# Softmax attention on one core: scores in three single PSUM banks, row maxima in three, exponentials 512 wide

## The chip, the core and the metric

The program runs on one core of one Trainium2 chip. A core has five engines with an instruction stream each: TensorE (PE, matrix multiplications and transposes), VectorE (DVE), ScalarE (ACT), GpSimd (POOL) and SyncE (SP, which issues the DMAs here). They wait for each other by semaphores. TensorE writes its results to PSUM, which has 8 banks of 512 fp32 words for each of 128 partitions, and VectorE and ScalarE read them there. The metric is the device time of the whole program in microseconds (us), less is better.

## The reference, cut to what matters

Four blocks follow one another on x of 2048 rows by 128 columns. Only the first, a softmax attention with 16 heads of width 8, is touched by the change:

```
x = x + _L0_attn_a_ref(_layernorm(x), w_qkv, w_out, b_out)
x = x + _L0_ffn_ref(...)          # six layers, local attention and MLP
x = x + _L0_attn_b_ref(...)       # linear attention
x = x + _L0_ffn_ref(...)          # the six layers again

def _L0_attn_a_ref(x, w_qkv, w_out, b_out):
    q, k, v = ...                 # x @ w_qkv, split in 16 heads of width 8
    q = _apply_rope(q, cos, sin)
    k = _apply_rope(k, cos, sin)
    scores = jnp.einsum('bhqd,bhkd->bhqk', q, k) / math.sqrt(D_HEAD)
    probs = jax.nn.softmax(scores, axis=-1)
    out = jnp.einsum('bhqk,bhkd->bhqd', probs, v)
    return out.transpose(...).reshape(b, t, d) @ w_out + b_out
```

Each head therefore has a matrix of 2048 by 2048 scores, whose rows each have their maximum subtracted before the exponential.

## The kernel before

`softmax_attention` makes the score matrix of each head twice. The first pass has the queries on the partitions: `scores_for_max` (L528) multiplies 128 queries by 512 keys into a bank of `ps_max`, and `maximum` (L413, on DVE) reduces it to one column. 64 such pairs, m = 0 to 63, make a head; `negate` (L418) turns the maxima into extra rows of the query operand, so that the second pass yields scores with the maximum already taken off. The second pass has the keys on the partitions: `scores` (L533) multiplies 128 keys by 512 queries, again 64 matmuls i = 0 to 63 in each head. ACT takes the exponential (L340) into `pex`, and `values` (L543) multiplies that by the values of the head, which adds up both the output and the denominator in the bank `ps_o`. An eighth bank, `ps_t`, serves the transposes of operands (`first`, `second`), which ACT copies out (L328, L333), and of the sums (`turn_sums`).

A head is 32 steps, n = 0 to 31. Two steps belong to one tile of 128 keys, kt = n // 2. In this text the two steps of a tile are called a group, so a head has groups 0 to 15. PE's stream in a group, written out by hand in `head` (L562), is: a maximum matmul, two scores, two maximum matmuls, two scores, a maximum matmul, the four `values` matmuls of the previous key tile. We call the scores of a group s1 to s4 and its maxima m1 to m4. The maxima belong to a later head: up to n = 25 to the next one (from its twelfth pair on), from n = 26 on to the one after that. In groups 8 to 11 the odd step (n = 17, 19, 21, 23, table `FIRST`) ends with eight transposes of the operands of head h + 2, and ACT copies them after its exponentials of that step. Steps 29 and 30 (`SECOND`) do the same for the query operand of head h + 1. Step 5 ends with `turn_sums`; on DVE `sums(h-1)` stands ahead of the maxima of step 2, `negate` ahead of those of step 26 and `outputs(h-1)` behind those of step 6.

What sets the pace between the engines is the number of free PSUM banks. `ps_max` has two banks, so matmul m waits until DVE has reduced m - 2 (L529). `ps_s` has two buffers of two banks. ACT reads one buffer, 1024 columns, with one instruction, and a pair of score matmuls waits for the exponential of the pair two steps back (L536). `pex` has two buffers, one for each key tile in work, and an exponential waits for the `values` of two tiles back (L339).

Head 0 and heads 13 to 15 are written out; heads 1 to 12 are three rounds of a hardware loop with four heads each (L192), in which the numbers that the engines wait for are computed in registers. Ahead of head 0 stands a preparation in which the 64 maxima of head 0 and the first 12 of head 1 are made with nothing beside them (L592 and L597). In head 14 the maxima end with step 25 and there are no `FIRST` transposes; in head 15 there are no maxima at all.

Of the kernel before, what the change touches and what calls it, by code (L numbers as in the profile page):

```python
# [7 lines left out]
F32 = mybir.dt.float32  # L8
BF16 = mybir.dt.bfloat16
ALU = mybir.AluOpType  # L10
ACT = mybir.ActivationFunctionType
AX = mybir.AxisListType

P = 128
D = 128
N = 2048
NT = N // P
# [14 lines left out]
NG = NT // GT  # L32
# [66 lines left out]
def softmax_attention(nc, tag, x_in, w_qkv, w_out, b_out, consts, x_out, xf, xa):  # L99


    with ExitStack() as ctx:
# [6 lines left out]
            sems.append(ctx.enter_context(nc.semaphore(f"{tag}_{name}")))  # L109
            return sems[-1]  # L110

        ps_s = [ctx.enter_context(nc.psum_tensor(f"{tag}_scores{i}", [P, 2, 512], F32)) for i in range(2)]
        ps_max = [ctx.enter_context(nc.psum_tensor(f"{tag}_max{i}", [P, 512], F32)) for i in range(2)]
        ps_o = ctx.enter_context(nc.psum_tensor(f"{tag}_sums", [P, 512], F32))
        ps_t = ctx.enter_context(nc.psum_tensor(f"{tag}_turned", [P, 512], F32))
        quarter = [ps_s[i // 2][:, i % 2, :] for i in range(4)]

        GQ = GT * P
        wqkv = sb("wqkv", [P, 3 * D])
# [22 lines left out]
        stackT = sb("stackT", [P, 4, 2, N], BF16)  # L142
        v_head = sb("v_head", [P, 2, NT, VW])
        maxima = sb("maxima", [P, NT, 4])
        neg = sb("neg", [P, 3, NT])
        pex = sb("pex", [P, 2, NG, GQ])
# [18 lines left out]
        own = {e: sem(f"own_{e}") for e in ("pool",)}  # L165

        PASS, STEPS = 4 * NT, 2 * NT


        EARLY = 12  # L170
# [125 lines left out]

        @block.scalar
        def _(act):
            act.sem_inc(act_ex, 2)

            def put_xT(g):
                act.wait_ge(pe_xT, g + 1)
                if g >= 2:
                    act.wait_ge(pe_qkv, g - 1)
                act.copy(xnT[:, g % 2, :, :], ps_t[:].rearrange("p (s q) -> p s q", s=GT)).then_inc(act_xT, 1)

            put_xT(0)
            for g in range(NG):
                if g + 1 < NG:
                    put_xT(g + 1)  # L310
                act.wait_ge(pe_qkv, g + 1)
                if g >= 2:
                    act.wait_ge(pl_t1, 2 * g - 2)
                    act.wait_ge(dv_t2, 4 * g - 4)
                for s in range(GT):
                    last = act.copy(qk[:, g % 2, :, s, :], quarter[s][:, 0:2 * D].rearrange("p (k d) -> p k d", k=2))
                last.then_inc(act_qk, 1)
                for s in range(GT):
                    last = act.copy(v_all[:, g * GT + s, :], quarter[s][:, 2 * D:3 * D])
                last.then_inc(act_v, 1)  # L320

            act.wait_ge(ld_c, 80)
            act.copy(ident_bf[:], ident[:]).then_inc(act_ident, 1)

            def first(h, slot, n):

                act.wait_ge(pe_first, 4 * h + n + 1)
                act.copy(stackT[:, slot, 1 - n // 2, 1024 * (n % 2):1024 * (n % 2) + 1024], ps_t[:].bitcast(BF16)).then_inc(act_first, 1)  # L328

            def second(h, slot, n):  # L330

                act.wait_ge(pe_second, 2 * h + n + 1)
                act.copy(stackT[:, slot, 0, 1024 * n:1024 * n + 1024], ps_t[:].bitcast(BF16)).then_inc(act_second, 1)  # L333

            def head(h, u):
                for n in range(STEPS):
                    kt, j = n // 2, n % 2
                    act.wait_ge(pe_s, STEPS * h + (n + 1))
                    act.wait_ge(pe_pv, NT * h + (kt + 1))  # L339
                    act.activation(pex[:, kt % 2, 2 * j:2 * j + 2, :], ps_s[j][:], ACT.Exp).then_inc(act_ex, 1)  # L340
                    if n in FIRST and exists(h, 2):
                        first(h + 2, (u + 2) % 4, FIRST[n])
                    if n in SECOND and exists(h, 1):
                        second(h + 1, (u + 1) % 4, SECOND[n])

            for h in range(2):
                for n in range(4):
                    first(h, h, n)
            for n in range(2):
                second(0, 0, n)  # L350
            all_heads(act, head)
            for g in range(NG):
                act.wait_ge(pe_aT, g + 1)
                if g >= 2:
                    act.wait_ge(pe_y, g - 1)
                act.copy(aoT[:, g % 2, :, :], ps_t[:].rearrange("p (s q) -> p s q", s=GT)).then_inc(act_aT, 1)

        @block.vector
        def _(dve):
            dve.sem_inc(dv_max, 2)  # L360
            dve.sem_inc(dv_os, 1)

            def norm_stats(k, g):
# [49 lines left out]
            def maximum(h, m):  # L413

                dve.wait_ge(pe_max, PASS * h + (m + 1))
                dve.tensor_reduce(maxima[:, m // 4, m % 4:m % 4 + 1], ps_max[m % 2][:], AX.X, ALU.max).then_inc(dv_max, 1)  # L416

            def negate(h, p):  # L418

                dve.wait_ge(dv_max, PASS * h + (PASS + 2))  # L420
                dve.tensor_reduce(neg[:, 0, :], maxima[:], AX.X, ALU.max, negate=True).then_inc(dv_neg, 1)
                dve.wait_ge(pe_first, 4 * h + 4)
                for i in range(3):
                    dve.wait_ge(dv_neg, 3 * h + (i + 1))
                    at = stack[:, p, 0, :, 72 + i]
                    dve.tensor_copy(at, neg[:, i, :]).then_inc(dv_negp, 1)
                    if i < 2:
                        dve.wait_ge(dv_negp, 3 * h + (i + 1))
                        dve.tensor_tensor(neg[:, i + 1, :], neg[:, i, :], at, ALU.subtract).then_inc(dv_neg, 1)
# [49 lines left out]
        def _(pe):  # L479
# [46 lines left out]
                transposes(p, 0, n).then_inc(pe_second, 1)  # L526

            def scores_for_max(h, slot, m):  # L528
                pe.wait_ge(dv_max, PASS * h + (m + 1))  # L529
                pe.matmul(ps_max[m % 2][:], stackT[:, slot, 0, P * (m // 4):P * (m // 4) + P],  # L530
                          stackT[:, slot, 1, GQ * (m % 4):GQ * (m % 4) + GQ], start=True, stop=True).then_inc(pe_max, 1)

            def scores(h, slot, n):  # L533

                kt, j = n // 2, n % 2
                pe.wait_ge(act_ex, STEPS * h + (n + 1))  # L536
                for e in range(2):
                    g = 2 * j + e
                    last = pe.matmul(ps_s[j][:, e, :], stackT[:, slot, 1, P * kt:P * kt + P],  # L539
                                     stackT[:, slot, 0, GQ * g:GQ * g + GQ], start=True, stop=True)  # L540
                last.then_inc(pe_s, 1)

            def values(h, p, kt):  # L543

                pe.wait_ge(act_ex, STEPS * h + (2 * kt + 4))
                if kt == 0:
                    pe.wait_ge(dv_os, h + 1)
                for g in range(NG):
                    last = pe.matmul(ps_o[VW * g:VW * g + VW, :], v_head[:, p, kt, :], pex[:, kt % 2, g, :],  # L549
                                     start=(kt == 0), stop=(kt == NT - 1), tile_position=(0, VW * g))  # L550
                last.then_inc(pe_pv, 1)
# [1129 lines left out]
```

## Time and profile before

| | |
|---|---|
| median of 3 runs | 5906.45 us (5892.85 to 5911.36) |
| profiled execution | 5901.95 us, its span 5900.1 us |
| granted TensorE clock, mean of the span | 0.955 |
| softmax attention, maxima of the preparation | 80.75 to 139 us of the span |
| softmax attention, the 16 heads | 139.8 to 993.4 us of the span |
| PE, DVE, ACT busy in the whole span | 87%, 75%, 65% |
| DVE maxima (L416) | 1024 of 686 ns |
| ACT exponentials (L340) | 512 of 1026 ns |

All times in the rows below are counted from the start of the span. A duration that a row gives for PE is that of one matmul from its start to its last write, and matmuls overlap: what a matmul costs PE is the distance between two starts. PEld is the loading of the weights ahead of a matmul. The rest of the program, from about 1000 us to the end, is code that the change doesn't touch.

### The profile page before, as it was taken

How to read it: one execution, taken by the hardware profiler on the slowest of the kernel's cores; microseconds unless marked ns; L12 is line 12 of the kernel's file. 1: busy time of each engine (PE TensorE's matmuls, PEld its weight loads, DVE VectorE, ACT ScalarE, POOL GpSimd, SP SyncE). 2: the span in 40 equal slices, each digit the busy share in tenths (PEclk: the TensorE clock that was granted, in tenths of full speed). 3: DMA queues.
4: the chain of work that ended last, by engine and by line, in shares of the span. 5: the costliest groups of instructions: out<-in, count | busy, mean ns of one | idle time of the engine just before them, and what ended most of it. 6: DMA issues, size and time to landing. Idle time of an engine off the chain costs nothing. (4 is left out here: it accounts for less than half of the span.)

```text
span 5900.1 us, 135041 instructions
## 1 busy us (share of the span) xinstructions
PE 5113.0 (87%) x38884; PEld 3411.9 (58%) x38884; DVE 4421.2 (75%) x8097; ACT 3864.6 (65%) x11648; POOL 2938.9 (50%) x2878
## 2 busy tenths in 40 slices
PE   5999997898988989989889677989989889898897
PEld 1223222566666666666666455666666666666665
DVE  7777775786876868868778546868868778687785
ACT  1666665775776757757667405757757677577675
POOL 3000000665665656656566306656656566566564
PEclk6999999999999999999999868999999999999999
DMA  0000001212222221121221202122222221212223
GB/s 12 1 1 1 1 1 38 60 48 70 52 58 58 52 70 47 48 73 48 68 54 47 75 9 82 48 69 53 60 57 49 69 52 47 73 49 60 59 51 85
DMA packets 332293, 288.23 MB, mean 49 GB/s; under 512 B 149102, under 2 KB 290708, under 8 KB 329748
## 3 DMA queue, kind: packets, MB, share of 16 engines
q1 hardware_dynamic: 331028, 282.33, 18.6%
q8 instruction: 222, 3.64, 0.3%
q14 instruction: 275, 2.25, 0.1%
q10 hardware_dynamic: 768, 0.02, 0.0%
HBM read 100.81 MB, written 30.41 MB: 22 GB/s over the span
## 5 line engine op out<-in xcount | busy, mean ns | idle before, releaser
L416 DVE TENSOR_REDUCE a_maxima<-a_max 128x1 f32<-128x512 f32 x1024 | 652.2, 686 | 195.8 <-PE a_max L530 191.8
L985 ACT ACTIVATE g_ex<-g_bank,g_nmx 128x96 f32<-128x96 f32 x1536 | 501.4, 338 | 345.3 <-DVE g_nmx L1067 345.3
L985 ACT ACTIVATE f_ex<-f_bank,f_nmx 128x96 f32<-128x96 f32 x1536 | 501.4, 338 | 343.1 <-DVE f_nmx L1067 343.1
L340 ACT ACTIVATE a_pex<-a_scores 128x1024 f32<-128x1024 f32 x512 | 517.1, 1026 | 217.4 <-PE a_scores L539 208.7
L920 POOL TENSOR_TENSOR f_rn<-f_sg,f_minus_half 128x8 f32<-128x8 f32 x384 | 640.1, 1667 | 32.0
L920 POOL TENSOR_TENSOR g_rn<-g_sg,g_minus_half 128x8 f32<-128x8 f32 x384 | 639.7, 1666 | 32.0
L925 POOL TENSOR_TENSOR f_qr<-f_t 128x512 f32<-128x512 f32 x384 | 547.7, 1426 | 14.8 <-DVE f_t L1086 13.1
L925 POOL TENSOR_TENSOR g_qr<-g_t 128x512 f32<-128x512 f32 x384 | 537.2, 1399 | 14.8 <-DVE g_t L1086 13.1
L1162 PE MATMUL g_bank<-g_wqkv,g_xT 128*128 128x512 f32 x768 | 427.7, 640 | 87.2 <-DVE g_qh L1077 62.1
L1162 PE MATMUL f_bank<-f_wqkv,f_xT 128*128 128x512 f32 x768 | 427.5, 639 | 86.6 <-DVE f_qh L1077 61.7
L530 PE MATMUL a_max<-a_stackT 128*128 128x512 bf16 x1024 | 410.9, 402 | 57.1 <-DVE a_maxima L416 26.2
L1061 DVE TENSOR_TENSOR g_pn<-g_ex,g_rd 128x384 f32<-128x384 f32 x384 | 426.7, 1111 | 13.1
L917 POOL TENSOR_SCALAR g_sg<-g_ss 128x8 f32<-128x8 f32 x384 | 92.4, 241 | 649.1 <-DVE g_ss L1073 649.1
L917 POOL TENSOR_SCALAR f_sg<-f_ss 128x8 f32<-128x8 f32 x384 | 92.3, 240 | 645.7 <-DVE f_ss L1073 645.7
L1061 DVE TENSOR_TENSOR f_pn<-f_ex,f_rd 128x384 f32<-128x384 f32 x384 | 393.3, 1024 | 13.1
L1067 DVE TENSOR_REDUCE f_nmx<-f_bank 128x4 f32<-128x384 f32 x384 | 212.1, 552 | 254.5 <-PE f_bank L1180 254.5
L1180 PEld LDWEIGHTS f_bank<-f_kT,f_qbd 128*128 128x128 f32 x3072 | 392.9, 192 | 8.0 <-issue 4.0
L1180 PEld LDWEIGHTS g_bank<-g_kT,g_qbd 128*128 128x128 f32 x3072 | 392.9, 192 | 8.0 <-issue 4.0
L1180 PE MATMUL f_bank<-f_kT,f_qbd 128*128 128x96 f32 x3072 | 394.6, 272 | 0.0
L1180 PE MATMUL g_bank<-g_kT,g_qbd 128*128 128x96 f32 x3072 | 394.6, 272 | 0.0
L1067 DVE TENSOR_REDUCE g_nmx<-g_bank 128x4 f32<-128x384 f32 x384 | 211.3, 550 | 227.6 <-PE g_bank L1180 227.6
L273 POOL COPY a_v_head<-a_v_all 128x128 f32 (+1 forms) x16 | 4.6, 290 | 738.3 <-PE a_sums L549 738.3
(235 smaller groups left out, 13205.3 us busy)
## 6 DMA issues: line engine op xcount, KB each, us to landing
f_vw<-f_vt SPq DMA_DIRECT2D x96, 384.0 KB, 4.3
g_vw<-g_vt SPq DMA_DIRECT2D x96, 384.0 KB, 4.3
f_vw<-f_vt SPq DMA_DIRECT2D x96, 256.0 KB, 3.6
g_vw<-g_vt SPq DMA_DIRECT2D x96, 256.0 KB, 3.6
f_vw<-f_vt SPq DMA_DIRECT2D x96, 128.0 KB, 2.3
g_vw<-g_vt SPq DMA_DIRECT2D x96, 128.0 KB, 2.3
f_wqkv<-in_f_Wqkv_dram SPq DMA_DIRECT2D x7, 1536.0 KB, 7.3
g_wqkv<-in_f_Wqkv_dram SPq DMA_DIRECT2D x7, 1536.0 KB, 9.4
```

What stands on the lines that cost most here:

```text
L273: pool.tensor_copy(v_head[:, p, :, 0:AD], one(v_all, h)).then_inc(pl_vh, 1)
L340: act.activation(pex[:, kt % 2, 2 * j:2 * j + 2, :], ps_s[j][:], ACT.Exp).then_inc(act_ex, 1)
L416: dve.tensor_reduce(maxima[:, m // 4, m % 4:m % 4 + 1], ps_max[m % 2][:], AX.X, ALU.max).then_inc(dv_max, 1)
L530: pe.matmul(ps_max[m % 2][:], stackT[:, slot, 0, P * (m // 4):P * (m // 4) + P], stackT[:, slot, 1, GQ * (m % 4):GQ * (m % 4) + GQ], start ...
L917: pool.tensor_scalar(sg[:, b, :], ss[:, b, :], 1e-24, None, ALU.max).then_inc(pl_sg, 1)
L920: pool.tensor_tensor(rn[:, b, :], sg[:, b, :], minus_half[:], ALU.pow).then_inc(pl_rn, 1)
L925: pool.tensor_tensor(qr[:, 1 - b, :], t1[:, 1 - b, :], t2[:, 1 - b, :], ALU.add).then_inc(pl_qr, 1)
L985: last = act.activation(ex[:, b, u, :], ps_s[:, KEYS * u:KEYS * u + KEYS], ACT.Exp, bias=nmx[:, b, u:u + 1], accum_out=sm[:, b, u:u + 1])
L1061: dve.tensor_tensor(pn[:, 1 - b, :, :], ex[:, 1 - b, :, :], rd[:, 1 - b, :].unsqueeze(2).broadcast_to([P, 4, KEYS]), ALU.mult).then_inc(dv ...
L1067: dve.tensor_reduce(nmx[:, b, :], ps_s[:, 0:4 * KEYS].rearrange("p (u c) -> p u c", u=4), AX.X, ALU.max, negate=True).then_inc(dv_max, 1)
L1162: pe.matmul(ps_qk[b][:], xT[:, q, :], wqkv[:, at:at + 512], start=True, stop=True).then_inc(pe_qkv, 1)
L1180: last = pe.matmul(ps_s[:, KEYS * u:KEYS * u + KEYS], qbd[:, j, blk, :], kT[:, j, BLK * blk:BLK * blk + KEYS], start=False, stop=(u == 3))
```

## The change

Eight banks are dealt out anew. The scores get three buffers of one bank (`ps_s`), the maxima get three (`ps_max`), the sums and the transposes keep one each. `quarter`, the four banks that the projections ahead of and behind the heads use, becomes the three score banks and the first maxima bank. ACT makes each exponential with an instruction of its own over 512 columns, 1024 instructions in place of 512, and each increments `act_ex`; so each of the 64 score matmuls of a head waits for the exponential that frees its bank, and each signals ACT by itself. Score i of a head uses bank i mod 3, so it waits for exponential i - 3; as 64 isn't a multiple of 3, `freed` gives the first three of a head their own numbers. The maxima go by the same function. The semaphores' starting values and the counts in `values` and `negate` follow. The numbers of instructions of PE's and DVE's work, and their sizes, stay.

```
@@ -109,11 +109,11 @@
             sems.append(ctx.enter_context(nc.semaphore(f"{tag}_{name}")))
             return sems[-1]
 
-        ps_s = [ctx.enter_context(nc.psum_tensor(f"{tag}_scores{i}", [P, 2, 512], F32)) for i in range(2)]
-        ps_max = [ctx.enter_context(nc.psum_tensor(f"{tag}_max{i}", [P, 512], F32)) for i in range(2)]
+        ps_s = [ctx.enter_context(nc.psum_tensor(f"{tag}_scores{i}", [P, 512], F32)) for i in range(3)]
+        ps_max = [ctx.enter_context(nc.psum_tensor(f"{tag}_max{i}", [P, 512], F32)) for i in range(3)]
         ps_o = ctx.enter_context(nc.psum_tensor(f"{tag}_sums", [P, 512], F32))
         ps_t = ctx.enter_context(nc.psum_tensor(f"{tag}_turned", [P, 512], F32))
-        quarter = [ps_s[i // 2][:, i % 2, :] for i in range(4)]
+        quarter = [ps_s[0][:], ps_s[1][:], ps_s[2][:], ps_max[0][:]]
 
         GQ = GT * P
         wqkv = sb("wqkv", [P, 3 * D])
@@ -166,6 +166,12 @@
 
         PASS, STEPS = 4 * NT, 2 * NT
 
+        AHEAD = 20 * PASS
+
+        def freed(h, i):
+
+            return PASS * h + ((0, -2, -1)[i] if i < 3 else i - 2)
+
 
         EARLY = 12
         LATE = (PASS - EARLY) // 2
@@ -296,7 +302,7 @@
 
         @block.scalar
         def _(act):
-            act.sem_inc(act_ex, 2)
+            act.sem_inc(act_ex, AHEAD)
 
             def put_xT(g):
                 act.wait_ge(pe_xT, g + 1)
@@ -334,10 +340,12 @@
 
             def head(h, u):
                 for n in range(STEPS):
-                    kt, j = n // 2, n % 2
-                    act.wait_ge(pe_s, STEPS * h + (n + 1))
-                    act.wait_ge(pe_pv, NT * h + (kt + 1))
-                    act.activation(pex[:, kt % 2, 2 * j:2 * j + 2, :], ps_s[j][:], ACT.Exp).then_inc(act_ex, 1)
+                    kt = n // 2
+                    if n % 2 == 0:
+                        act.wait_ge(pe_pv, NT * h + (kt + 1))
+                    for i in (2 * n, 2 * n + 1):
+                        act.wait_ge(pe_s, PASS * h + (i + 1))
+                        act.activation(pex[:, kt % 2, i % NG, :], ps_s[i % 3][:], ACT.Exp).then_inc(act_ex, 1)
                     if n in FIRST and exists(h, 2):
                         first(h + 2, (u + 2) % 4, FIRST[n])
                     if n in SECOND and exists(h, 1):
@@ -357,7 +365,7 @@
 
         @block.vector
         def _(dve):
-            dve.sem_inc(dv_max, 2)
+            dve.sem_inc(dv_max, PASS)
             dve.sem_inc(dv_os, 1)
 
             def norm_stats(k, g):
@@ -413,11 +421,11 @@
             def maximum(h, m):
 
                 dve.wait_ge(pe_max, PASS * h + (m + 1))
-                dve.tensor_reduce(maxima[:, m // 4, m % 4:m % 4 + 1], ps_max[m % 2][:], AX.X, ALU.max).then_inc(dv_max, 1)
+                dve.tensor_reduce(maxima[:, m // 4, m % 4:m % 4 + 1], ps_max[m % 3][:], AX.X, ALU.max).then_inc(dv_max, 1)
 
             def negate(h, p):
 
-                dve.wait_ge(dv_max, PASS * h + (PASS + 2))
+                dve.wait_ge(dv_max, PASS * h + 2 * PASS)
                 dve.tensor_reduce(neg[:, 0, :], maxima[:], AX.X, ALU.max, negate=True).then_inc(dv_neg, 1)
                 dve.wait_ge(pe_first, 4 * h + 4)
                 for i in range(3):
@@ -526,23 +534,22 @@
                 transposes(p, 0, n).then_inc(pe_second, 1)
 
             def scores_for_max(h, slot, m):
-                pe.wait_ge(dv_max, PASS * h + (m + 1))
-                pe.matmul(ps_max[m % 2][:], stackT[:, slot, 0, P * (m // 4):P * (m // 4) + P],
+                pe.wait_ge(dv_max, freed(h + 1, m))
+                pe.matmul(ps_max[m % 3][:], stackT[:, slot, 0, P * (m // 4):P * (m // 4) + P],
                           stackT[:, slot, 1, GQ * (m % 4):GQ * (m % 4) + GQ], start=True, stop=True).then_inc(pe_max, 1)
 
             def scores(h, slot, n):
 
-                kt, j = n // 2, n % 2
-                pe.wait_ge(act_ex, STEPS * h + (n + 1))
-                for e in range(2):
-                    g = 2 * j + e
-                    last = pe.matmul(ps_s[j][:, e, :], stackT[:, slot, 1, P * kt:P * kt + P],
-                                     stackT[:, slot, 0, GQ * g:GQ * g + GQ], start=True, stop=True)
-                last.then_inc(pe_s, 1)
+                kt = n // 2
+                for i in (2 * n, 2 * n + 1):
+                    g = i % NG
+                    pe.wait_ge(act_ex, AHEAD + freed(h, i))
+                    pe.matmul(ps_s[i % 3][:], stackT[:, slot, 1, P * kt:P * kt + P],
+                              stackT[:, slot, 0, GQ * g:GQ * g + GQ], start=True, stop=True).then_inc(pe_s, 1)
 
             def values(h, p, kt):
 
-                pe.wait_ge(act_ex, STEPS * h + (2 * kt + 4))
+                pe.wait_ge(act_ex, PASS * h + (AHEAD + 4 * kt + 4))
                 if kt == 0:
                     pe.wait_ge(dv_os, h + 1)
                 for g in range(NG):
```

In head 0 PE's instructions of the first two steps stand as follows before (the digit behind `a_max` and `a_scores` is the buffer; a `scores` buffer holds two banks here).

```order
L530 MATMUL a_max0<-a_stackT 128x512 [waits a_dv_max,a_pl_vh,a_act_second]
L539 MATMUL a_scores0<-a_stackT 128x512 [waits a_act_ex]
L539 MATMUL a_scores0<-a_stackT 128x512
L530 MATMUL a_max1<-a_stackT 128x512 [waits a_dv_max]
L530 MATMUL a_max0<-a_stackT 128x512 [waits a_dv_max]
L539 MATMUL a_scores1<-a_stackT 128x512 [waits a_act_ex]
L539 MATMUL a_scores1<-a_stackT 128x512
L530 MATMUL a_max1<-a_stackT 128x512 [waits a_dv_max]
```

And the same place in the changed kernel, where each buffer is one bank.

```order
L538 MATMUL a_max0<-a_stackT 128x512 [waits a_dv_max,a_pl_vh,a_act_second]
L547 MATMUL a_scores0<-a_stackT 128x512 [waits a_act_ex]
L547 MATMUL a_scores1<-a_stackT 128x512 [waits a_act_ex]
L538 MATMUL a_max1<-a_stackT 128x512 [waits a_dv_max]
L538 MATMUL a_max2<-a_stackT 128x512 [waits a_dv_max]
L547 MATMUL a_scores2<-a_stackT 128x512 [waits a_act_ex]
L547 MATMUL a_scores0<-a_stackT 128x512 [waits a_act_ex]
L538 MATMUL a_max0<-a_stackT 128x512 [waits a_dv_max]
```

No matmul changes its place in PE's order. The third maximum no longer goes into the bank of the first, the fourth score goes into the bank of the first score of the same group, and every score has a wait.

ACT's instructions at the start of head 0, behind the last two copies of the preparation, before:

```order
L333 COPY a_stackT<-a_turned 128x1024 [waits a_pe_second] x2
L340 ACTIVATE a_pex<-a_scores0 128x1024 [waits a_pe_pv,a_pe_s]
L340 ACTIVATE a_pex<-a_scores1 128x1024 [waits a_pe_pv,a_pe_s]
L340 ACTIVATE a_pex<-a_scores0 128x1024 [waits a_pe_pv,a_pe_s]
L340 ACTIVATE a_pex<-a_scores1 128x1024 [waits a_pe_pv,a_pe_s]
```

And in the changed kernel:

```order
L339 COPY a_stackT<-a_turned 128x1024 [waits a_pe_second] x2
L348 ACTIVATE a_pex<-a_scores0 128x512 [waits a_pe_s,a_pe_pv]
L348 ACTIVATE a_pex<-a_scores1 128x512 [waits a_pe_s]
L348 ACTIVATE a_pex<-a_scores2 128x512 [waits a_pe_s]
L348 ACTIVATE a_pex<-a_scores0 128x512 [waits a_pe_s]
L348 ACTIVATE a_pex<-a_scores1 128x512 [waits a_pe_s,a_pe_pv]
L348 ACTIVATE a_pex<-a_scores2 128x512 [waits a_pe_s]
```

Four instructions take the place of two in each group, and the wait for `values` stands at the first of the four alone.

## Rows read from the trace of the kernel before

**Rows 1.** Stages: preparation, head 3, head 15.

```profile
core 0: us, PE busy (x) PEld busy (x) DVE busy (x) ACT busy (x) POOL busy (x), PEclk, DMA share, GB/s
80.75:139.00 58.25, 47.48 (x93) 9.49 (x93) 50.34 (x83) 2.61 (x3) 2.86 (x7) 0.50 0.00 0
...
302.40:357.00 54.60, 51.25 (x309) 16.48 (x308) 42.85 (x74) 37.73 (x39) 3.15 (x8) 1.00 0.00 1
...
959.60:993.40 33.80, 32.79 (x194) 6.64 (x194) 1.24 (x3) 30.96 (x32) 0.00 (x0) 1.00 0.00 1
```

**Rows 2.** Waits, 240 to 820 us: total us, times, longest us.

```profile
PEld a_max L530 <- DVE a_maxima L416: 247.4, 424, 1.5
```

**Rows 3.** Timeline, group 5 of head 3: start us, us long, engine, instruction, [idle before].

```profile
324.26 0.39 PE L530 MATMUL a_max<-a_stackT 128*128 128x512 bf16 x1
...
324.48 0.59 PE L539 MATMUL a_scores<-a_stackT 128*128 128x512 bf16 x2
324.68 2.53 DVE L416 TENSOR_REDUCE a_maxima<-a_max 128x1 f32<-128x512 f32 x4 [0.61 <-PE a_max L530]
...
324.91 0.91 PE L530 MATMUL a_max<-a_stackT 128*128 128x512 bf16 x2
325.19 2.12 ACT L340 ACTIVATE a_pex<-a_scores 128x1024 f32<-128x1024 f32 x2 [1.02 <-PE a_scores L539]
...
325.66 0.59 PE L539 MATMUL a_scores<-a_stackT 128*128 128x512 bf16 x2
...
326.09 0.38 PE L530 MATMUL a_max<-a_stackT 128*128 128x512 bf16 x1
...
326.40 1.07 PE L549 MATMUL a_sums<-a_pex,a_v_head 128*32 128x512 f32 x8
...
327.40 0.39 PE L530 MATMUL a_max<-a_stackT 128*128 128x512 bf16 x1
```

**Rows 4.** ACT by line and shape: busy us, mean ns | idle before us.

```profile
L340 ACT ACTIVATE a_pex<-a_scores 128x1024 f32<-128x1024 f32 x512 | 517.1, 1026 | 217.4 <-PE a_scores L539 208.7
...
L976 ACT ACTIVATE g_sq<-g_bank 128x512 f32<-128x512 f32 x384 | 235.3, 613 | 112.8 <-PE g_bank L1162 112.8
...
L328 ACT COPY a_stackT<-a_turned 128x1024 bf16<-128x1024 bf16 x64 | 64.8, 1012 | 76.9 <-PE a_turned L504 76.9
...
L305 ACT COPY a_xnT<-a_turned 128x512 f32<-128x512 f32 x4 | 2.5, 635 | 12.3 <-PE a_turned L487 12.3
...
L356 ACT COPY a_aoT<-a_turned 128x512 f32<-128x512 f32 x4 | 2.3, 585 | 7.6 <-PE a_turned L608 7.6
```

**Rows 5.** Timeline of group 9 of head 3, behind a set of transposes.

```profile
331.00 0.38 PE L530 MATMUL a_max<-a_stackT 128*128 128x512 bf16 x1
...
331.20 1.01 ACT L328 COPY a_stackT<-a_turned 128x1024 bf16<-128x1024 bf16 x1 [0.74 <-PE a_turned L504]
...
332.11 1.95 ACT L340 ACTIVATE a_pex<-a_scores 128x1024 f32<-128x1024 f32 x2
...
334.13 0.62 PE L504 MATMUL a_turned<-a_ident_bf,a_stack 128*128 128x128 bf16 x8
...
334.58 0.38 PE L530 MATMUL a_max<-a_stackT 128*128 128x512 bf16 x1
```

**Rows 6.** Timeline of PE: starts of groups 1 and 2, of 13 and 14.

```profile
304.62 0.39 PE L530 MATMUL a_max<-a_stackT 128*128 128x512 bf16 x1
...
308.06 0.39 PE L530 MATMUL a_max<-a_stackT 128*128 128x512 bf16 x1
...
344.89 0.39 PE L530 MATMUL a_max<-a_stackT 128*128 128x512 bf16 x1
...
348.76 0.39 PE L530 MATMUL a_max<-a_stackT 128*128 128x512 bf16 x1
```

**Rows 7.** Timeline of PE in the preparation.

```profile
98.22 1.21 PE L530 MATMUL a_max<-a_stackT 128*128 128x512 bf16 x2 [0.18 <-DVE a_maxima L416]
...
101.01 1.21 PE L530 MATMUL a_max<-a_stackT 128*128 128x512 bf16 x2 [0.18 <-DVE a_maxima L416]
```

## The prediction

> **What bounds the kernel now.** I read the table of stages first [rows 1]. A head takes 54.60 us, in which PE is busy for 51.25, DVE for 42.85 and ACT for 37.73. No engine but PE comes near the length of the head, so the question is what PE waits for. The list of waits names it [rows 2]: in 580 us the weight loads of the maxima matmuls ended their idle time 424 times on a DVE reduction, far ahead of anything else on PE. (The 247.4 us there are idle time of the weight loader and not of the matmuls, so they are no price.) The price stands in the timeline of one ordinary group [rows 3]. It begins with m1 at 324.26, and the next begins at 327.40: 3.14 us. PE's starts lie 0.22 us apart (two scores in 0.43), 0.31 ahead of `values`, and 1.00 behind it. One step is longer. The two maxima merged at 324.91 last 0.91 together and one lasts 0.39, so m3 starts at 325.43, which is 0.52 after m2 in place of 0.22. It waits for the reduction of m1, which starts at 324.68 and lasts 0.69 (0.686 in the kernel's mean): to 325.37, and PE goes 0.06 later. So 0.30 us of each ordinary group is a wait for one of two maxima banks; without it a group is 2.84 us.
>
> ACT isn't tight there. Its two exponentials take 2.12 us of the 3.14, the second starting 0.04 after the last score ended (325.66 + 0.59 = 326.25, against 325.19 + 2.12 - 1.02 = 326.29).
>
> **The change, part by part.** *Third maxima bank.* m3 no longer waits for m1 but for the reduction of the previous group's m4. The four reductions of a group follow each other every (2.53 - 0.69) / 3 = 0.61 us, 2.4 us in a group of 2.84, so DVE keeps up and the 0.30 goes. What is late next is to be looked for at the scores.
>
> *Exponentials of 512 columns.* The trace has no exponential of that size. The copy of 1024 columns takes 1012 ns and one of 512 takes 585 [rows 4], which is 0.83 ns for each column; 1026 - 427 gives 0.60 us. Back to back, the two behind the copy take 1.95 us at 1.03 each [rows 5], so the second starts 0.92 after the first; 512 columns less make this 0.49. Bounds: 0.585, the shortest operation of this width in rows 4, and 1.026, the whole exponential as it is. The squares of 512 columns take 613 and the copies of the preparation 635, both close to the lower end, so I take 0.60. ACT then needs 4 x 0.49 to 4 x 0.60 = 2.0 to 2.4 us in a group, which is still under 2.84: 512 additional instructions cost nothing as long as PE doesn't wait for one.
>
> The Trainium skill speaks against this part. "Advanced Engine Details and Errata", section TRN2 Errata, says that each ScalarE instruction exposes its access latency as a bubble, and advises large tiles and reading several PSUM banks with one instruction, which is what the change gives up. "ScalarE: Activation LUTs", section What ACT_TABLE_LOAD costs, gives 186 ns + 0.833 ns for each column, 0.613 us here and 93 ns less in series: by an estimate from that page each round trip below is 0.013 longer, about 3 us over the heads.
>
> *Three score banks, each with its own wait.* s4 goes into the bank of s1 of its own group. Without any stall s4 stands 0.22 + 5 x 0.22 = 1.31 us after m1 (rounded steps: 0.22, 0.44, 0.65, 0.87, 1.09, 1.31). The bank comes free like this: s1 starts at 0.22 and lasts 0.38, ACT starts 0.04 later and takes 0.60, and PE goes 0.06 later, at 1.30. That is just in time, so an ordinary group is 2.84, but with no reserve: each further 0.01 in this trip is 0.01 in each group. The wait at each score costs PE nothing in itself. Maxima matmuls have such a wait and a register operation of their own now, and where the bank is free they stand 0.22 apart like the rest [rows 3].
>
> *Groups behind a copy (9 to 12).* Here the trip is longer. The copy starts 0.20 after m1 and the next exponential 0.91 after the copy [rows 5]. s4 can go at 0.20 + 0.91 + 0.60 + 0.06 = 1.77, 0.46 late. In groups 9 to 11 the transposes then close a ring: from the copy's start 1.57 to s4, 0.22 to m4, 0.31 to `values`, 1.00 to the transposes, 0.62 for these, 0.04 to the next copy, 3.76 us in all. Before it is 334.58 - 331.00 = 3.58. Each of the three costs 0.18, and group 12 costs 0.46 - 0.30 = 0.16.
>
> *The rest of a head.* Groups 0, 2 to 8 and 14 gain 0.30 each, 2.70. Group 1, where DVE copies the sums ahead of its maxima, takes 308.06 - 304.62 = 3.44 [rows 6] and becomes 2.84, since the bank it waits for is freed 0.6 earlier: 0.60. Group 13 has `negate` ahead of its maxima and takes 348.76 - 344.89 = 3.87, that is a stall of 3.87 - 2.84 = 1.03 at m3. The stall moves to m4, 0.65 further on in PE's order, and 0.38 is left: 0.65 gained. At the end of a head s64 and s1 of the next head share a bank. From the first `SECOND` copy ACT needs 0.91 + 2 x 0.49 + 0.91 + 0.49 + 0.60 = 3.89 until the bank is free, while PE reaches s1 after 1.01 + 0.06 + 0.46 + 3 x 0.22 + 0.31 + 1.00 + 0.22 = 3.72: 0.23 lost. (0.46 is what eight transposes cost PE, 334.58 - 334.13.) Sum of a head: -2.70 - 0.60 - 0.65 + 3 x 0.18 + 0.16 + 0.23 = -3.02. Heads 0 to 13: -42.3.
>
> *Head 14* has no `FIRST`. Groups 0 to 12 gain 12 x 0.30 + 0.60 = 4.2. Groups 13 to 15 have no maxima and lose about 0.4 + 0.4 + 0.6 to the trip of the next item: -2.8.
>
> *Head 15* has scores, exponentials and `values` alone. It takes 33.80 us [rows 1], ACT busy for 30.96, 2.11 a group. With three banks s4 must be followed by `values` and then by the next s1 before ACT gets work: 0.31 + 1.00 + 0.38 + 0.04 + 0.60 + 0.06 = 2.39, since the next s4 needs that exponential. 16 x 2.39 = 38.2: +4.4.
>
> *Preparation.* Two banks, four matmuls every 101.01 - 98.22 = 2.79 us [rows 7], so 0.70 for each maximum, at a granted clock of 0.50 [rows 1], the 1.2 GHz level. The trip of one bank is 0.61 (matmul) + 0.04 + 0.69 + 0.06 = 1.40. Over three banks this is 0.47, below DVE's own 0.61. 76 x 0.09 = 6.8 gained.
>
> Sum: -42.3 - 2.8 + 4.4 - 6.8 = **-47.5 us**. The profiled execution took 5901.95 us, 1.85 around its span of 5900.1; with the change 5854. The median of the runs is 4.5 higher, 5906.45, and gives 5859. I forecast **5858 us**. The other four stages, from 1000 us on, have the same code.
>
> **Rivals.** *The score trip replaces the bank wait (short gain).* The ordinary group has 0.01 in reserve. If the handoffs with their register operations are longer than I took them (the first exponential in rows 3 starts 0.12 after the scores ended, 325.07 to 325.19, where the second takes 0.04), each group's trip grows by 0.08. Then an ordinary group is 2.91, rows behind copies 3.84, head 15 2.47 a group: 0.08 x 15 groups x 15 heads = 18 back, plus 1.3 in head 15: a gain of 28, **5878**. For it: two handoffs of different length in the same row. Against it: the longer one belongs to an instruction that has two waits, and the changed kernel puts the `values` wait, long fulfilled, ahead of it.
>
> *ACT becomes the bound (slower).* If an exponential of 512 columns costs nearly as much as one of 1024, since it has a fixed cost, a bubble and a wait of its own, ACT sets the pace. A head has 64 of them and 6 copies of 1.01. At 0.80 us each this is 51.2 + 6.1 = 57.3 against 54.60, +2.7 in 15 heads; head 15 becomes 51.2 against 33.80, +17.4; the preparation gives 6.8 back: +51, **5957**. It decides from about 0.75 us on: 15 heads x (48.0 + 6.1 - 54.6) + 14.2 - 6.8 = 0. For it stands the first rule of the skill above. Against it: everything of 512 columns in rows 4 lies at 0.59 to 0.64.
>
> *The third maxima bank gives nothing (no change).* DVE's next reduction, not the bank, could hold m3. It would have to be busy, and it idles 0.61 us ahead of m1's reduction in each group [rows 3]. Should half of the stall stay, as a wait at m3 or m4, 0.15 x 11 groups x 15 heads = 25 of the 47.5 is lost, **5881**. With all of it left the price of the copies and of head 15 stands alone against the preparation, and the time is about 5904.
>
> **How the numbers follow.** Forecast 0.75. Short gain 0.13. No change 0.07, ACT as the bound 0.05. The forecast's own range, from exponentials of 0.585 to 0.635 and a few us of scatter between runs, is 5846 to 5870; with the short gain the range is **5845 to 5886**. Faster by more than 0.3% (18 us, about what a measurement tells from no change) means under 5889: nearly all of the first two, 0.87. Within 0.3%: 0.08. Slower: 0.05.
>
> **What would show it.** In the changed profile an ordinary group of head 3 should last 2.84 us, with m3 0.22 after m2; the exponentials should have a mean of 0.60 and stand 0.49 apart behind a copy. Groups 9 to 11 should take 3.76, with PE waiting for ACT at s4. Head 3 should last 51.6, head 15 38, the maxima of the preparation 0.61 each. The prediction is wrong if the exponentials take over 0.65, if ordinary groups show PE waiting at s4, or if m3 still starts 0.5 after m2.

## The result and the profile after

| | before | changed |
|---|---|---|
| median | 5908.9 us (4 runs, 5892.85 to 5916.06) | 5856.93 us (4 runs, 5853.8 to 5868.74) |
| profiled execution | 5901.95 us, span 5900.1 | 5853.8 us, span 5852.0 |
| first exponential of head 0 | 139.77 us | 131.66 us |
| end of head 15 | 993.4 us | 945.2 us |
| from there to the end of the span | 4906.7 us | 4906.8 us |

The ratio of the changed kernel to the one before is 0.9913, 95% interval 0.9901 to 0.9926: it is faster, by 52 us in the medians and by 48.1 in the two profiled spans. All of the latter lies in the softmax attention.

The stages, to be read against [rows 1]: maxima of the preparation, head 3, head 15 of the changed kernel.

```profile
core 0: us, PE busy (x) PEld busy (x) DVE busy (x) ACT busy (x) POOL busy (x), PEclk, DMA share, GB/s
80.72:131.00 50.28, 41.55 (x93) 9.20 (x92) 46.24 (x82) 2.61 (x3) 2.87 (x7) 0.64 0.00 0
286.00:337.40 51.40, 49.63 (x309) 16.58 (x308) 43.05 (x74) 38.55 (x70) 3.17 (x8) 1.00 0.00 1
905.80:945.20 39.40, 34.31 (x195) 7.68 (x193) 1.24 (x3) 33.02 (x64) 0.00 (x0) 1.00 0.00 1
```

A head of the loop went from 54.6 to 51.4 us, and PE, busy for 49.63 of them, has 1.8 us without work left in place of 3.4. Head 15 is the stage that became longer, from 33.80 to 39.40.

The waits of the changed kernel from 232 to 780 us (total us, times, longest us) answer to [rows 2].

```profile
PEld a_max L538 <- DVE a_maxima L424: 87.4, 116, 0.8
...
PEld a_scores L547 <- ACT a_pex L348: 73.3, 168, 0.8
...
PE a_scores L547 <- ACT a_pex L348: 12.3, 40, 0.3
```

The maxima's wait for DVE is down from 424 times to 116. The scores' wait for ACT, which isn't among the longest waits of before, is now the second longest of those of PE and its weight loader. As before, the first two lines are idle time of the weight loader and no price; the last one, 40 times 0.3 us, is PE's own and comes from the groups behind a copy, shown below.

One ordinary group of the changed kernel (group 5 of head 2, start and length in us), against [rows 3]:

```profile
248.61 0.39 PE L538 MATMUL a_max<-a_stackT 128*128 128x512 bf16 x1
...
248.84 0.59 PE L547 MATMUL a_scores<-a_stackT 128*128 128x512 bf16 x2
...
249.25 2.06 ACT L348 ACTIVATE a_pex<-a_scores 128x512 f32<-128x512 f32 x4 [0.77 <-PE a_scores L547]
249.27 0.59 PE L538 MATMUL a_max<-a_stackT 128*128 128x512 bf16 x2
...
249.70 0.60 PE L547 MATMUL a_scores<-a_stackT 128*128 128x512 bf16 x2
...
251.44 0.39 PE L538 MATMUL a_max<-a_stackT 128*128 128x512 bf16 x1
```

It lasts 251.44 - 248.61 = 2.83 us, where it was 3.14. The pair m2, m3 now lasts 0.59 and not 0.91: both start 0.22 apart, and no wait is left there. The pair s3, s4 lasts 0.60 where a pair without a wait lasts 0.59, so s4 goes just in time. The exponentials have a mean of 606 ns:

```profile
L348 ACT ACTIVATE a_pex<-a_scores 128x512 f32<-128x512 f32 x1024 | 531.6, 606 | 157.7 <-PE a_scores L547 157.7
```

Group 9 of head 3, which stands behind a copy, has turned into the ring of the prediction; compare [rows 5]. First PE, then ACT.

```profile
311.79 0.38 PE L538 MATMUL a_max<-a_stackT 128*128 128x512 bf16 x1
...
313.56 0.39 PE L547 MATMUL a_scores<-a_stackT 128*128 128x512 bf16 x1 [0.31 <-ACT a_pex L348]
...
315.55 0.38 PE L538 MATMUL a_max<-a_stackT 128*128 128x512 bf16 x1
```

```profile
311.99 1.01 ACT L334 COPY a_stackT<-a_turned 128x1024 bf16<-128x1024 bf16 x1 [0.78 <-PE a_turned L512]
312.90 2.07 ACT L348 ACTIVATE a_pex<-a_scores 128x512 f32<-128x512 f32 x4
315.75 1.01 ACT L334 COPY a_stackT<-a_turned 128x1024 bf16<-128x1024 bf16 x1 [0.77 <-PE a_turned L512]
```

From copy to copy it is 3.76 us, and from m1 to m1 too, where before it was 3.58. s4 starts at 313.56, 1.77 after m1 and 1.57 after the start of the copy.

Head 15, where the loss is (PE and ACT):

```profile
920.57 0.82 PE L547 MATMUL a_scores<-a_stackT 128*128 128x512 bf16 x3
921.06 2.06 ACT L348 ACTIVATE a_pex<-a_scores 128x512 f32<-128x512 f32 x4 [0.39 <-PE a_scores L547]
...
921.71 0.39 PE L547 MATMUL a_scores<-a_stackT 128*128 128x512 bf16 x1 [0.32 <-ACT a_pex L348]
...
923.03 0.82 PE L547 MATMUL a_scores<-a_stackT 128*128 128x512 bf16 x3
```

Three scores go out, the fourth waits for the exponential of the first, and `values` stands between it and the next three: 2.46 us a group. Here s1, the first of the three and 0.39 long, ends at 920.57 + 0.39 = 920.96, and ACT starts 0.10 later. In the group of head 2 above s1 ends at 248.84 + 0.38 = 249.22, and ACT starts 0.03 later (0.04 by the trace's unrounded times).

### The profile page after: what moved, and what is told of

Its sections match the earlier page's. It is cut to its first block and busy times, and to the rows that moved or that the text cites. A ratio compares the mean times of both kernels' runs of the same rounds, so it can differ in the third digit from the quotient of the medians.

```text
span 5852.0 us, 136065 instructions
## 1 busy us (share of the span) xinstructions
PE 5077.2 (87%) x38884; PEld 3412.5 (58%) x38884; DVE 4411.0 (75%) x8097; ACT 3883.6 (66%) x12160; POOL 2947.4 (50%) x2878
## 5 line engine op out<-in xcount | busy, mean ns | idle before, releaser
L348 ACT ACTIVATE a_pex<-a_scores 128x512 f32<-128x512 f32 x1024 | 531.6, 606 | 157.7 <-PE a_scores L547 157.7
L538 PE MATMUL a_max<-a_stackT 128*128 128x512 bf16 x1024 | 365.4, 394 | 14.3 <-DVE a_maxima L424 7.5
```

The costliest lines, as they stand in the source:

```text
L348: act.activation(pex[:, kt % 2, i % NG, :], ps_s[i % 3][:], ACT.Exp).then_inc(act_ex, 1)
L538: pe.matmul(ps_max[m % 3][:], stackT[:, slot, 0, P * (m // 4):P * (m // 4) + P], stackT[:, slot, 1, GQ * (m % 4):GQ * (m % 4) + GQ], start ...
```

## Experiments

The theory is that of the prediction: the third maxima bank brings the gain; exponentials of 512 columns are free in themselves; but with three score banks, the trip of a bank (a score matmul, an exponential and the two handoffs, which are the times from the end of one engine's instruction to the start of the next engine's) must fit into what PE has to do until it needs the bank again, and where it doesn't, PE waits at s4. The main rival says that the narrower exponentials, each freeing its bank early, bring the gain. Each comparison has its own runs of the kernel before: median 5899.67 us (14 runs) for the first four, 5910.21 (18 runs) for the last two. So ratios are compared across them, and single groups by the traces.

### Two maxima banks in the changed kernel

```
-        ps_max = [... for i in range(3)]      # scores keep three banks
+        ps_max = [... for i in range(2)]
-                pe.wait_ge(dv_max, freed(h + 1, m))
-                pe.matmul(ps_max[m % 3][:], ...
+                pe.wait_ge(dv_max, PASS * h + (m + 1))
+                pe.matmul(ps_max[m % 2][:], ...
```

> The changed kernel with two maxima banks again and the eighth bank unused; scores and exponentials stay as changed. Theory (the gain is the third maxima bank): an ordinary group goes from 2.83 back to 3.13 us with m3 0.52 behind m2, groups 9 to 11 stay at 3.76, a head of the loop takes 55.2 in place of 51.4, the maxima of the preparation 0.70 each in place of 0.60. 14 x 3.8 + 4 + 7 = 64 us more than the changed kernel: 5921, which is 12 slower than the kernel before. Rival (the narrower exponentials, each freeing its own bank, bring the gain): ordinary groups stay under 2.95 and the time under 5875.

Measured: 5926.22 us, ratio to before 1.0042 (1.0028 to 1.0056), slower than before by some 25 us. Head 3 and an ordinary group of it, PE's rows:

```profile
305.40:360.90 55.50, 51.25 (x304) 16.46 (x308) 43.27 (x74) 39.63 (x70) 3.17 (x8) 1.00 0.00 1
```

```profile
321.52 0.59 PE L547 MATMUL a_scores<-a_stackT 128*128 128x512 bf16 x2 [0.16 <-issue]
321.95 0.91 PE L538 MATMUL a_max<-a_stackT 128*128 128x512 bf16 x2
...
324.66 0.59 PE L547 MATMUL a_scores<-a_stackT 128*128 128x512 bf16 x2
```

The pair m2, m3 lasts 0.91 again and the group 324.66 - 321.52 = 3.14. The heads as a whole, from the first exponential to the last, take 876.3 us against 813.6 with three maxima banks and 853.7 before. The rival falls: with all of the change but the third maxima bank the kernel is slower than before, by 22.6 us in the heads. This is the price of having three score banks in place of four; the next run takes the narrow exponentials out of it.

### Narrow exponentials alone, over four score banks

```
-        ps_s = [... [P, 2, 512] ... for i in range(2)]
+        ps_s = [... [P, 512] ... for i in range(4)]
-                    act.activation(pex[:, kt % 2, 2 * j:2 * j + 2, :], ps_s[j][:], ...
+                    for i in (2 * n, 2 * n + 1):
+                        act.wait_ge(pe_s, PASS * h + (i + 1))
+                        act.activation(pex[:, kt % 2, i % NG, :], ps_s[i % 4][:], ...
-                pe.wait_ge(act_ex, STEPS * h + (n + 1))          # once for two scores
+                    pe.wait_ge(act_ex, PASS * h + (AHEAD + i - 3))   # for each
```

> The kernel before with the other half of the change alone: exponentials of 512 columns over four single score banks, a wait for each score, two maxima banks. Theory: with a fourth bank no score waits and the narrower instructions hide under PE; ordinary groups stay at 3.14 because m3 still waits for the reduction of m1; head 15 about 1 us shorter; in all 5905 (5898 to 5912), no change. Rival 1 (freeing banks sooner is itself worth something): 5885 or less. Rival 2 (512 more instructions on ACT cost something): over 5920, with ACT late in groups 9 to 12.

Measured: 5903.7 us, ratio 1.0006 (0.9996 to 1.0015). Heads 3 and 15, and the maxima pair of an ordinary group:

```profile
301.70:356.30 54.60, 50.53 (x304) 16.47 (x308) 42.87 (x74) 39.75 (x71) 3.17 (x8) 1.00 0.00 1
959.40:991.50 32.10, 31.28 (x191) 7.70 (x193) 1.24 (x3) 31.70 (x65) 0.00 (x0) 1.00 0.01 1
```

```profile
318.20 0.91 PE L534 MATMUL a_max<-a_stackT 128*128 128x512 bf16 x2
```

Head 3 is what it was, and the heads as a whole take 852.5 us against 853.7. The 512 additional instructions of ACT and the 512 additional waits of PE cost nothing, and they win nothing either, but for head 15, in which ACT was busy for 30.96 of 33.8 us: it takes 32.1, where about 1 us less was expected. Both rivals fall. This kernel and the one of the run above differ in the fourth score bank alone, and in the heads by 876.3 - 852.5 = 23.8 us: groups 9 to 11 of head 3 take 3.59 here and 3.76 there, head 15 32.1 and 39.4.

### The copy behind the first exponential of the next step

```
                     for i in (2 * n, 2 * n + 1):
                         act.wait_ge(pe_s, PASS * h + (i + 1))
                         act.activation(...)
-                    if n in FIRST and exists(h, 2):
-                        first(h + 2, (u + 2) % 4, FIRST[n])
+                        if i == 2 * n and n - 1 in FIRST and exists(h, 2):
+                            first(h + 2, (u + 2) % 4, FIRST[n - 1])
```

> The changed kernel, in which ACT makes each FIRST copy behind the first exponential of the next step and not ahead of it; nothing else moves. Theory (groups 9 to 12 are a ring copy, exponential of s1, s4, values, transposes, copy): s4's bank is free in time again, groups 9 to 11 go from 3.76 to PE's own 3.30 and group 12 keeps its length or loses a little; head 3 goes from 51.4 to 49.7, 14 heads x 1.65 = 23 us: 5834. Rival (these groups are held by the transposes' own bank or by ACT's total work): they stay at 3.7 or more, 5850 to 5860.

Measured: 5830.72 us, ratio 0.9885 (0.9869 to 0.9902). Group 9 of head 3, PE and then ACT:

```profile
306.22 0.38 PE L538 MATMUL a_max<-a_stackT 128*128 128x512 bf16 x1
...
307.30 0.59 PE L547 MATMUL a_scores<-a_stackT 128*128 128x512 bf16 x2
...
309.49 0.38 PE L538 MATMUL a_max<-a_stackT 128*128 128x512 bf16 x1
```

```profile
306.85 0.60 ACT L348 ACTIVATE a_pex<-a_scores 128x512 f32<-128x512 f32 x1 [1.21 <-PE a_scores L547]
307.34 1.01 ACT L334 COPY a_stackT<-a_turned 128x1024 bf16<-128x1024 bf16 x1
308.23 1.60 ACT L348 ACTIVATE a_pex<-a_scores 128x512 f32<-128x512 f32 x3
```

The group takes 309.49 - 306.22 = 3.27 us in place of 3.76, and the pair s3, s4 has no wait. Head 3 takes 49.8, where 49.7 were expected, and the heads 790.9 against 813.6. So the ring is shown, and it was the order on ACT alone that closed it: the copy that nobody needs soon stood ahead of the exponential that frees s4's bank. (Counted from m1 to m1 as here, group 12 becomes shorter too, from 3.30 to 3.01, and group 13 longer, from 3.21 to 3.35.)

### Longer exponentials, in the changed kernel and in the one before

```
-                        act.activation(..., ps_s[i % 3][:], ACT.Exp)
+                        act.activation(..., ps_s[i % 3][:], ACT.Exp, bias=no_bias[:])   # a column of zeros
     # and at the start a memset of that column and one wait for it
```

> The changed kernel with exponentials made longer by a cost of their own: each takes its bias, a zero, from a column in SBUF and not as a constant. The sums are the same. Theory (s4's bank is free just in time, so there is no reserve): whatever x an exponential becomes longer, each ordinary group, each of groups 9 to 11 and each group of head 15 becomes longer by x. With x of about 0.09 us an ordinary group is 2.92, groups 9 to 11 3.85, head 15 2.55 a group; 0.09 x 15 groups x 15 heads + 1.5 = 22 us more than the changed kernel, 5879. Rival (ACT has slack, it is busy for only 70% of the heads, so its instructions may be longer for nothing): 5857.

> The kernel before with the same longer exponentials (of 1024 columns, bias from a column in SBUF). Theory: with four score banks the exponentials have a reserve of several tenths of a us, ordinary groups stay at 3.14 and groups 9 to 11 at 3.59; only head 15, where ACT is the bound, gets 32 x 0.09 = 3 us longer: 5903 to 5910. Rival (longer exponentials cost the same in both kernels, so the loss of the other run isn't due to the missing bank): 20 us more, 5920 or over.

Measured: the changed kernel with longer exponentials 5893.45 us, ratio 0.9976 (0.9967 to 0.9986) against 0.9913 without; the kernel before with them 5915.09, ratio 1.0006 (0.9995 to 1.0017). Both medians lie above the times expected, by 14 and 5 us; the median of the kernel before had itself risen by 10.5 in this comparison, so the theory is judged by the heads. In the trace of the changed one the exponentials have a mean of 692 ns, 0.09 more than 606, and an ordinary group is this:

```profile
305.72 0.59 PE L550 MATMUL a_scores<-a_stackT 128*128 128x512 bf16 x2 [0.16 <-ACT a_pex L351]
...
306.58 0.69 PE L550 MATMUL a_scores<-a_stackT 128*128 128x512 bf16 x2
...
308.64 0.59 PE L550 MATMUL a_scores<-a_stackT 128*128 128x512 bf16 x2
```

The pair s3, s4 lasts 0.69: s4 waits for 0.10. The group is 308.64 - 305.72 = 2.92, so the 0.09 of one exponential appear once in the group, in full. Head 3 takes 53.03, and the heads 837.8 against 813.6, 24.2 more where 22 were expected. (The rest of the difference of the medians isn't from the heads, see the last section.) In the kernel before, with exponentials of 1117 ns:

```profile
319.39 0.59 PE L542 MATMUL a_scores<-a_stackT 128*128 128x512 bf16 x2 [0.16 <-ACT a_pex L343]
319.82 0.91 PE L533 MATMUL a_max<-a_stackT 128*128 128x512 bf16 x2
...
322.53 0.59 PE L542 MATMUL a_scores<-a_stackT 128*128 128x512 bf16 x2
```

The group is 3.14 as ever and heads 1 to 3 take 54.56. Only head 15 reacts, 35.4 against 33.8, which is 1.6 us where 3 were expected. The same 0.09 us cost 24 us in the heads with three score banks (837.8 against 813.6) and 2 with four (855.7 against 853.7).

### All together

```
-        SECOND = {29: 0, 30: 1}
+        SECOND = {28: 0, 30: 1}
     # written-out heads: act.wait_ge(pe_s, ...) first, then act.wait_ge(pe_pv, ...)
+        def score_bank(h, i):
+            return (ps_s + ps_max)[i % 6][:] if last_head(h) else ps_s[i % 3][:]
     # and the moved copy of the run above
```

> As the run with the moved copy, and three more steps: the SECOND transposes and copies at steps 28 and 30 in place of 29 and 30 (so that PE doesn't wait for the first copy ahead of the second transposes); in the written-out heads the wait for values ahead of the exponential is put where the scores' wait is the last one (0.06 us in each group of heads 0, 13, 14, 15); and head 15, which has no maxima, uses the three maxima banks for scores too. Theory: 23 us by the copy, 15 heads x 0.5 = 7 by SECOND, about 2.5 by the waits, 39.4 - 33 = 6 in head 15: 5857 - 38 = 5819. Rival (only the copy counts, PE being full otherwise): 5834.

Measured: 5815.51 us, ratio 0.9862 (0.9846 to 0.9879), the fastest of all, 1.4% under the kernel before. Heads 3 and 15:

```profile
279.00:328.40 49.40, 48.28 (x305) 16.78 (x309) 42.85 (x74) 38.58 (x71) 3.15 (x8) 1.00 0.00 1
873.50:905.60 32.10, 31.09 (x192) 7.72 (x193) 1.24 (x3) 31.65 (x64) 0.00 (x0) 1.00 0.00 1
```

Head 15 goes from 39.4 to 32.1 us with three banks more, the order of its waits included. A loop head goes from 49.8 to 49.3 by `SECOND`. Step three, the order of two waits, shows in an ordinary group of head 13, which is written out. First the run with the moved copy alone, then this one (starts of m1):

```profile
801.65 0.39 PE L538 MATMUL a_max<-a_stackT 128*128 128x512 bf16 x1
...
804.54 0.39 PE L538 MATMUL a_max<-a_stackT 128*128 128x512 bf16 x1
```

```profile
795.16 0.39 PE L547 MATMUL a_max<-a_stackT 128*128 128x512 bf16 x1
...
797.99 0.39 PE L547 MATMUL a_max<-a_stackT 128*128 128x512 bf16 x1
```

2.89 us became 2.83, the length that such a group has in the loop. The other two steps don't touch this group.

The brackets [waits ...] of the `order` lists name the waits of an instruction in the reverse of their order in the program, and so does the expectation when it puts the scores' wait last: in the program this run puts it first, as the lines above say. The kernel before has that order everywhere, and in its written-out heads ACT starts 868.91 - (868.28 + 0.60) = 0.03 us behind the scores (head 13):

```profile
868.28 0.60 PE L539 MATMUL a_scores<-a_stackT 128*128 128x512 bf16 x2
...
868.91 1.02 ACT L340 ACTIVATE a_pex<-a_scores 128x1024 f32<-128x1024 f32 x1 [0.94 <-PE a_scores L539]
```

So the 0.06 us a group in the written-out heads came with the change itself, which exchanged the two waits.

## Why the prediction was right, point by point

The sum of the terms was -47.5 us and the time forecast at 5858; 5856.93 was measured, and the profiled spans differ by 48.1. The medians differ by 52.0. That sum and time came out within a few us is in part luck: the runs of the changed kernel scatter over 15 us, and some of the terms were off in opposite directions. The terms, by the two profiled executions:

| term | forecast | measured |
|---|---|---|
| preparation | -6.8 | -8.1 |
| heads 0 to 13 | -42.3 | -43.7 |
| head 14 | -2.8 | -2.0 |
| head 15 | +4.4 | +5.6 |

Group by group the mechanism is as forecast. In head 3, from m1 to m1, group 1 is shorter by 0.62 us (0.60 forecast), groups 2 to 8 and 14 by 0.31 each (0.30), group 13 by 0.66 (0.65), groups 9 to 11 are longer by 0.17 or 0.18 each (0.18) and group 12 by 0.17 (0.16). Group 0 wins only 0.05, since s1 waits behind the `SECOND` copies (0.30 - 0.23 forecast).

*Third maxima bank.* The wait of 0.30 us went in full, and DVE kept up. Two maxima banks bring it back, 0.91 for the pair and 3.14 for the group.

*The exponential of 512 columns* was taken at 0.60 from two copies and has 0.606. That 512 more of them cost nothing where the banks suffice is shown by the run with four score banks. The Trainium skill's rule against it ("Advanced Engine Details and Errata", TRN2 Errata: large tiles, several banks with one instruction) describes a cost that ACT does have, 33.02 us busy in head 15 against 30.96, but in 15 of the 16 heads ACT had room for it, and in head 15 the run with four score banks is shorter than before all the same. By an estimate from the Trainium skill's page "ScalarE: Activation LUTs" (What ACT_TABLE_LOAD costs) such an exponential takes 0.613 us, and the page gives about 93 ns for a pointer operand; the trace has 0.606, and 692 - 606 = 86 ns for the bias column.

*The trip s1 to s4* was worked out at 1.30 against a place of 1.31. The pair of 0.60 says that it just fits. The run with longer exponentials says that nothing was left over: 0.09 more in the exponential is 0.09 more in the group.

*Groups behind a copy.* 3.76 forecast and measured. Moving the copy takes the ring away.

*Group 13* was taken at 3.22, and the trace has 3.21. A head of the loop was forecast at 51.6 and takes 51.4, 3.16 less than before where 3.02 were forecast.

*Where sizes were off.* In head 15 the trip was taken at 2.39 and is 2.46: the handoff of 0.04 holds in the loop only. In the written-out heads ACT starts 0.10 after s1, and their ordinary groups take 2.89: there PE does wait at s4, for 0.06. So head 0 wins 1.97 and head 13 2.65 where 3.02 were forecast, and head 14 1.96 where 2.8 were. That was the mechanism of the "short gain" rival, which I had argued away for all heads, and it holds in four of sixteen, in the other ones than I would have thought. The argument against it misread the rows: in the kernel before both exponentials of a tile have the two waits and not only the one that starts late. That the changed kernel puts the `values` wait ahead did shorten the handoff in the loop (0.12 before, 0.04 now), and in the written-out heads it made it longer.

*Heads 0 to 13* were forecast at -42.3 and took -43.7. The loop heads won more than forecast and heads 0 and 13 less, and a part has nothing to do with the banks. Wherever the hardware loop starts a new round, behind heads 4 and 8, PE stands still for 1.95 and 2.40 us in the trace of before and for 3.53 and 3.12 in that of the change (2.0 to 3.6 in all eight traces). The first of them, before and changed:

```profile
412.62 0.39 PE L530 MATMUL a_max<-a_stackT 128*128 128x512 bf16 x1 [1.95 <-issue]
```

```profile
391.54 0.39 PE L538 MATMUL a_max<-a_stackT 128*128 128x512 bf16 x1 [3.53 <-issue]
```

In the trace of before the granted clock is 0.50 for 3.4 us shortly after each of the two, and heads 5 and 9 are 1.7 and 1.4 us longer than the other loop heads; in that of the change it stays at 1.00. Together the longer stops and the clock make up 1.3 of the 43.7 us, and no run varies them on purpose.

*The preparation* won more than its 6.8. The distance of two reductions went from 0.695 to 0.598 us, 7.1 for the 76 maxima. The other 1.0 lies at the end: head 0's first exponential starts 0.06 us behind the last reduction and not 1.03, since PE no longer waits for DVE as long ahead of the first scores, and since the exponential needs one score and not two.

*The rival without a gain* was priced too low. 25 us lost from 5858 give 5883 and not 5881, and with all of the stall left the time isn't 5904: two maxima banks in the changed kernel give 5926, some 25 above the kernel before.

The rival in which ACT becomes the bound needed 0.75 us an exponential; it has 0.606. The rival in which the third maxima bank gives nothing is excluded by the first experiment.

## What to carry to other kernels

Eight PSUM banks are a budget: read from the timeline which buffer's return PE waits for, and give it the bank, but write down the trip of the buffer that pays (matmul, handoff, reader, handoff) against the time that PE has for other work in it. Here the trip just fitted, and 0.09 us more in the exponential came back in full in each group. Splitting the wide instruction was free here, where its engine had room, and it is what made the odd number of banks possible. Once a buffer is short, what stands ahead of its release in the reader's queue counts: a copy that nobody was waiting for cost 23 us, by standing one exponential too early. And the order of two waits on one instruction is part of a change: here it moved along unnoticed and cost 0.06 us in each group of the written-out heads.

## What the runs showed of the hardware

- Two waits on one ACT instruction, named in the order of the program: in the written-out heads ACT starts 0.10 us after the score matmul's end where the long fulfilled wait for `values` comes first and the scores' wait last, and 0.04 where the scores' wait comes first. Exchanging the two lines gave 0.06 us a group. In the loop, where the numbers waited for are in registers, it is the other way round: 0.04 with the scores' wait last, and 0.12 with it first in the kernel before, there only at the first exponential of a tile and not at the second. Why is open.
- The granted clock in the preparation: with two maxima banks (reductions 0.70 us apart) it was at the 1.2 GHz level throughout (0.50), before the change and in the first experiment. With three (0.60 apart) it rose to 2.4 GHz for parts of the stage and fell again (0.64 on average), while the distance stayed the same, so the distance alone doesn't tell the level. The rise was worth nothing there, because DVE, busy all the time, set the pace at either level; in these rows of the changed kernel it makes a maximum every 0.60 us at both:

```profile
82.70:92.90 10.20, 6.66 (x18) 1.66 (x18) 10.20 (x18) 0.00 (x0) 0.00 (x0) 1.00 0.00 0
92.90:119.10 26.20, 24.99 (x42) 4.29 (x42) 26.18 (x44) 0.00 (x0) 0.00 (x0) 0.50 0.00 0
```

- A stop of PE doesn't decide the clock by its length alone: after the stops of 1.95 and 2.40 us between rounds of the loop in the kernel before it fell to 0.50 for 3.4 us, after those of 3.53 and 3.12 us in the changed kernel it didn't.
- The part of the program behind the heads, the same code in all kernels, took from 4900.4 to 4923.5 us in the profiled spans, and the median of the kernel before was 5899.67 us in one comparison and 5910.21 in another. Differences of medians under some 15 us can't be given to an edit here without the trace of the stage: of the 37 us between the changed kernel and the one with longer exponentials 24 are in the heads, 8 in that part of the two profiled spans.
